# A fused transformer block with routed experts: the end of full attention in another order, and the second experts' output scatters no longer ordered

## The reference, cut to what matters

```python
attn_out = _mha(x, in_proj_w, in_proj_b, out_proj_w, out_proj_b)
x = _layernorm(x + attn_out, ln1_g, ln1_b)
# _hier_moe: one expert of eight for each of the 4096 rows
gp = jax.nn.softmax(xt @ w_group + b_group, axis=-1)
ep = jax.nn.softmax(elog, axis=-1)            # 2 experts in each of 4 groups
flat_e = g_idx * EXPERTS_PER_GROUP + e_idx_local
combine = jax.nn.one_hot(flat_e, E) * (g_prob * e_prob)[:, None]
h = jax.nn.relu(jnp.einsum('td,edf->etf', xt, w1) + b1[:, None, :])
y = jnp.einsum('etf,efd->etd', h, w2) + b2[:, None, :]
out = jnp.einsum('te,etd->td', combine, y)
x = _layernorm(x + moe_out, ln2_g, ln2_b)     # and the block's input is added once more
```

## Time and profile before

| | |
|---|---|
| median of 3 runs | 2338.34 us (2334.56 to 2341.31) |
| profiled execution | 2331.83 us, its span 2330.0 us |
| mean granted TensorE clock | 0.946 of full speed |
| PE busy over the span | 1995.3 us, 86% |
| DVE, ACT, POOL busy | 64%, 53%, 49% |

### The profile page before, as it was taken

How to read it: one execution, slowest core, us unless ns; L and a number is a source line. 1 busy time by engine, 2 the same in 40 slices (tenths; PEclk the granted TensorE clock), 3 DMA queues, 4 the chain that set the end, 5 groups by cost and what they waited for, 6 DMA issues and landing times. The chain is left out here.

```text
span 2330.0 us, 36967 instructions
## 1 busy us (share of the span) xinstructions
PE 1995.3 (86%) x12360; PEld 1189.0 (51%) x12360; DVE 1484.8 (64%) x3224; ACT 1244.2 (53%) x2953; POOL 1141.1 (49%) x949
## 2 busy tenths in 40 slices
PE   7999999989999999975677995999999999764986
PEld 3555555555555555552245783444444444333875
DVE  4348777786868687775844654666777776453555
ACT  6676666666666666742112331566666666431432
POOL 2007566584747475673663534233344432144655
PEclk9999999999999999997798996899999999985999
DMA  8214453526200000005134653123233211214653
GB/s 285 58 56 156 143 158 123 178 96 213 70 24 1 20 1 19 1 17 146 54 113 129 186 174 88 48 72 84 60 84 89 68 54 32 69 44 145 218 188 114
DMA packets 195685, 226.07 MB, mean 97 GB/s; under 512 B 24173, under 2 KB 167021, under 8 KB 195370
## 3 DMA queue, kind: packets, MB, share of 16 engines
q1 hardware_dynamic: 146250, 149.48, 21.3%
q0 software_dynamic: 14880, 39.35, 5.5%
q10 hardware_dynamic: 34368, 34.87, 4.4%
HBM read 97.92 MB, written 114.46 MB: 91 GB/s over the span
## 5 line engine op out<-in xcount | busy, mean ns | idle before, releaser
L2043 DVE TENSOR_REDUCE m_mx<-ps 128x2 f32<-128x1024 f32 x256 | 313.3, 1224 | 191.6 <-PE ps L1978 189.1
L734 DVE CUSTOM_DVE_ANT_0 pb<-ps,bias,snl 128x128 f32<-128x128 f32 (+3 forms) x512 | 260.2, 546 | 226.6 <-PE ps L579 225.7
L852 POOL TENSOR_TENSOR prod<-qs,kvs 128x1024 f32<-128x1024 f32 x120 | 283.9, 2393 | 163.5 <-issue 142.3
L2113 ACT ACTIVATE m_pt<-ps 128x1024 f32<-128x1024 f32 x256 | 261.4, 1023 | 171.4 <-PE ps L1986 166.6
L852 POOL TENSOR_TENSOR prod<-sc,kvs 128x1024 f32<-128x1024 f32 x120 | 280.3, 2369 | 98.5 <-ACT sc L970 85.7
L930 ACT ACTIVATE pb<-pb,mst 128x129 f32<-128x129 f32 (+3 forms) x512 | 283.4, 560 | 19.1 <-DVE mst L734 17.0
L579 PE MATMUL ps<-kz,qT 64*128 64x128 f32 (+3 forms) x1024 | 186.3, 442 | 0.0
L590 PE MATMUL ps<-ident,pb 128*128 128x128 f32 x1280 | 179.3, 279 | 0.5 <-DVE mst L734 0.4
L864 DVE TENSOR_REDUCE sc<-prod 128x64 f32<-128x1024 f32 x128 | 152.2, 1209 | 42.0 <-POOL prod L852 41.7
L945 ACT ACTIVATE ptb<-ps 128x384 f32<-128x384 f32 (+1 forms) x256 | 135.4, 544 | 67.5 <-PE ps L590 67.1
L590 PEld LDWEIGHTS ps<-ident,pb 128*128 128x128 f32 x1280 | 140.4, 142 | 55.9 <-issue 43.5
(11 more groups left out here) (337 smaller groups left out, 4273.5 us busy)
## 6 DMA issues: line engine op xcount, KB each, us to landing
xh_scratch<-zh SPq DMA_DIRECT2D x32, 1032.0 KB, 9.7
xe_scratch<-zh ACTq DMA_DIRECT2D x32, 1024.0 KB
hw_w<-in_w SPq DMA_DIRECT2D x47, 512.0 KB
...
```

Source lines behind the costliest of these rows:

```text
L734: dv.tensor_tensor_reduce(pb.ap[:, j, SEG[t]:SEG[t] + n], rS.of(("S", b, p, t, j)).ap[:, 0:n], k.bias[:, h, CAUSAL[t]:CAUSAL[t + 1]], -1.0 ...
L852: e.tensor_tensor(out, one, two, ALU.mult).then_inc(*k.c.did(*product_done(step, b, t, u)))
L2043: dv.tensor_reduce(x.ap[:, t, 64 * half:64 * half + 64].rearrange("p (i r) -> p i r", i=2)[:, :, 2], score_ring(k, b, g, t, half).of((b, g ...
L2113: ac.activation(p.ap[:, 2 * half:2 * half + 2, :], k.qE.of((b, g, kt, half)).ap, ACT.Exp).then_inc(*did("m_exp", b, g, kt, half))
```

## The change: what it does

Four edits.

1. The order of steps in `last_rows`: the four `f_out` of batch 7 stand together, then its four `f_norm`, `h_turn` and `h_score`; only then follow `h_gate` 1 and `h_count` 1 (batch 6), and `h_back` of batch 7. Before, `h_gate` 1 stood behind the second `f_out`, and `h_score` of batch 7 behind `h_count` 1.
2. The scatter of slot n to the output waits for its own rows alone.
3. `hslots` neither moves the last tile of an expert back nor repeats the last slot: tiles start at whole multiples of 128 rows of their expert's list, and what lies behind the list's end are the zero rows, whose number is out of bounds, so that gather and scatter skip them. Six DVE instructions go. The scratch has 8 tiles more, and one more `clear` of 1 MB is issued in the first part.
4. In the fourth part, `h_more` stands behind the loads of the first three slots instead of ahead of them.

```diff
@@ -305,7 +305,7 @@
 
 FOLD_AT = 4
 
-HROWS = 6
+HROWS = E8 * CAP + (NS_H - NN + 1) * P
 
 
 def order_one():
@@ -502,9 +502,10 @@
             sync_rest(k, sp)
         elif step == "clear":
             w.wait_ge(at("zero", 1))
-            i, n = key[0], E8 * CAP // CLEARS
-            sp.dma_start(k.xhd[i * n:(i + 1) * n, :].rearrange("(n p) d -> p n d", p=P),
-                         k.zh[:, :].unsqueeze(1).broadcast_to([P, n // P, ROW])).then_inc(*did("d_zh", i))
+            n = E8 * CAP // CLEARS
+            for i in range(key[0], HROWS // n, CLEARS):
+                sp.dma_start(k.xhd[i * n:(i + 1) * n, :].rearrange("(n p) d -> p n d", p=P),
+                             k.zh[:, :].unsqueeze(1).broadcast_to([P, n // P, ROW])).then_inc(*did("d_zh", i))
         elif step == "x_last":
             for t in range(NT):
                 sp.dma_start(x1_tile(k, NB - 1, t), ins["x"][NB - 1, t * P:(t + 1) * P, :]).then_inc(*did("d_xl", t))
@@ -1742,9 +1743,9 @@
     some = lambda n: [next(lots) for _ in range(n)]
     out = [("h_score", b - 1)] + [("f_turn", b, t) for t in range(NT)] + [("h_back", b - 1)]
     out += [("f_bias", b, 2)] + some(3) + [("f_bias", b, 3)] + some(6) + [("f_out", b, 0)] + some(1)
-    out += [("f_out", b, 1), ("h_gate", 1), ("f_norm", b, 0)] + some(1)
-    out += [("f_out", b, 2), ("f_norm", b, 1)] + some(1) + [("f_out", b, 3), ("f_norm", b, 2), ("f_norm", b, 3)]
-    return out + [("h_turn", b), ("h_count", 1)] + list(lots) + [("h_scatter", n) for n in range(*HLOT[1])]
+    out += [("f_out", b, t) for t in (1, 2, 3)] + [("f_norm", b, 0)] + some(1) + [("f_norm", b, 1)] + some(1)
+    out += [("f_norm", b, 2), ("f_norm", b, 3), ("h_turn", b), ("h_score", b), ("h_gate", 1), ("h_count", 1), ("h_back", b)]
+    return out + list(lots) + [("h_scatter", n) for n in range(*HLOT[1])]
 
 
 def order_three():
@@ -1754,7 +1755,7 @@
     out += [("p_v", 0, 0), ("p_v", 0, 1), ("m_banks",)] + period(-1)
     for b in range(NB + 1):
         out += period(b)
-    out += [("h_score", NB - 1), ("h_back", NB - 1), ("h_gate", HLAST), ("h_count", HLAST)]
+    out += [("h_gate", HLAST), ("h_count", HLAST)]
     return out + [("h_scatter", n) for n in range(*HLOT[HLAST])] + [("h_slots",)]
 
 
@@ -2193,7 +2194,7 @@
 
 
 def order_four():
-    return [("h_more",)] + [("h_expert", j) for j in range(NS_H + 4)] + [("h_end",)]
+    return [("h_expert", 0), ("h_more",)] + [("h_expert", j) for j in range(1, NS_H + 4)] + [("h_end",)]
 
 
 def setup_four(k, nc, ins):
@@ -2207,7 +2208,6 @@
     k.hcum = [[e["v0"](f"h_cum{g}{i}", [P, n1 - n0, E8]) for i in range(3)] for g, (n0, n1) in enumerate(HLOT)]
     k.hmore = e["v0"]("h_more", [P, E8, NN])
     k.hin = e["v0"]("h_in", [P, NS_H, E8])
-    k.hin2 = e["q"]("h_in2", [P, NS_H, E8])
     k.htot = e["v0"]("h_tot", [P, HLAST + 4, E8])
     k.hte = e["v0"]("h_te", [P, 5, NS_H])
     k.hgix = e["v0"]("h_gix", [P, NS_H], I32)
@@ -2274,7 +2274,7 @@
                 if n < NS_H:
                     x = k.hxs.of(n)
                     w.wait_ge(at("hgix", 0), at("i_hsc", NN - 1), x.room)
-                    r = sp.value_load(k.hgix[0:1, n:n + 1], min_val=0, max_val=E8 * CAP - P)
+                    r = sp.value_load(k.hgix[0:1, n:n + 1], min_val=0, max_val=HROWS - P)
                     sp.dma_start(x.ap[:, :], k.xhd[bass.ds(r, P), :]).then_inc(*did(f"d_hxs{n % HX}", n))
                     t = k.w1.take(n, at("h_h", n, 3))
                     w.wait_ge(at("h_tei", 0), t.room)
@@ -2446,7 +2446,7 @@
 def hslots(k, dv, w):
 
     did = k.c.did
-    tot, nt, first, base = [k.htot[:, i, :] for i in range(HLAST, HLAST + 4)]
+    tot, nt, first = [k.htot[:, i, :] for i in range(HLAST, HLAST + 3)]
     n = HLOT[HLAST][1] - HLOT[HLAST][0]
     w.wait_ge(at("hc_more", HLAST))
     dv.tensor_tensor(tot, k.htot[:, HLAST - 1, :], k.inch[HLAST][:, n - 1, :], ALU.add).then_inc(*did("hs_tot", 0))
@@ -2460,24 +2460,16 @@
-    te, own, at_, end, slot = [k.hte[:, i, :] for i in range(5)]
-    dv.tensor_scalar(base[:, 0:1], nt[:, E8 - 1:E8], first[:, E8 - 1:E8], 1.0, ALU.add, ALU.subtract).then_inc(*did("hs_base", 0))
-    dv.scalar_tensor_tensor(tot, tot, 1.0, k.hplace[:, 0:E8], ALU.subtract, ALU.add).then_inc(*did("hs_tot", 4))
-    w.wait_ge(at("hs_base", 0))
-    dv.tensor_scalar(slot, k.hiota[:, :], base[:, 0:1], None, ALU.min).then_inc(*did("hs_slot", 0))
-    w.wait_ge(at("hs_slot", 0))
+    te, own, at_ = [k.hte[:, i, :] for i in range(3)]
+    slot = k.hiota[:, :]
-    w.wait_ge(at("hs_in", 0), at("hs_tot", 4))
+    w.wait_ge(at("hs_in", 0))
-    dv.tensor_tensor(k.hin2[:, :, :], k.hin[:, :, :], wide8(tot, NS_H), ALU.mult).then_inc(*did("hs_in2", 0))
-    w.wait_ge(at("hs_in2", 0))
-    dv.tensor_reduce(end, k.hin2[:, :, :], AX, ALU.max).then_inc(*did("hs_end", 0))
@@ -2486,9 +2478,7 @@
-    dv.scalar_tensor_tensor(own, te, float(CAP), at_, ALU.mult, ALU.add).then_inc(*did("hs_own", 3))
-    w.wait_ge(at("hs_own", 3), at("hs_end", 0))
-    dv.tensor_tensor(k.hgix[:, :], own, end, ALU.min).then_inc(*did("hgix", 0))
+    dv.scalar_tensor_tensor(k.hgix[:, :], te, float(CAP), at_, ALU.mult, ALU.add).then_inc(*did("hgix", 0))
@@ -2598,7 +2588,7 @@
             if 0 <= j - 4 < NS_H:
                 n = j - 4
 
-                w.wait_ge(at("h_res", n), at(f"i_out{(n - 1) % HZ}", n - 1) if n else None)
+                w.wait_ge(at("h_res", n))
                 po.indirect_dma_start(k.out.rearrange("b s d -> (b s) d"), bass.IndirectOffsetOnAxis(ap=k.hxs.of(n).ap[:, D + 1:D + 2].bitcast(I32), axis=0),
                                       k.hz.of(n).ap[:, :], None, bounds_check=NN * P - 1, oob_is_err=False).then_inc(*did(f"i_out{n % HZ}", n))
             if j < NS_H:
@@ -2629,7 +2619,7 @@
-        self.xhd = nc.dram_tensor("xh_scratch", [E8 * CAP, ROW], F32).ap()
+        self.xhd = nc.dram_tensor("xh_scratch", [HROWS, ROW], F32).ap()
```

## The result

| | before | after |
|---|---|---|
| median (4 runs each, on one chip) | 2336.45 us (2321.46 to 2341.31) | 2304.59 us (2297.53 to 2306.26) |
| ratio | | 0.987, 95% interval 0.9831 to 0.9909 |
| profiled execution, and its span | 2331.83, 2330.0 us | 2306.26, 2304.4 us |
| clock | 0.946 | 0.946 |

The change makes the kernel 31.9 us faster by the medians, where 40 were forecast (2298.0, range 2289 to 2314).

A forecast was written before the change was run, and what follows sets the result against it. Output scatters, each waiting for the previous landing, were taken to hold slots at 4.525 us against PE's 3.73. Terms 4.3 + 0 + 2.3 + 33.4 = 40.0 us off the 2338.3 us median gave 2298, range 2289 to 2314.

The forecast's parts named there:

- step 1: End of attention: with batch 6's gates behind batch 7's norms, batch 7's gates start 4.3 us earlier.
- Step 2: `hslots`: six small DVE instructions go, 3 us at most, but hidden beside batch 7's scatters; gain 0.
- Step 3: Fourth part's first loads: rows asked for 1.0 us earlier and landing 1.3 us sooner without the bias ahead; 2.3 us.
- step 4: Fourth part's slots: without ordered output scatters they run at PE's 3.734 us instead of 4.525; 33.4 us gained.
- first case: Fourth part: PE paces the slots, giving the full forecast of 2298 us; chance 0.62.
- third rival: End of attention: new order gains nothing, batch 6's counting delays batch 7 or DVE stops grow; 2302 us, chance 0.08.
- The lock: Slots: DVE's port lock stretches POOL; POOL or late transfers pace at 3.85 to 4.1 us; 2303 to 2312, chance 0.25.
- Crowding out: Slots: unordered scatters and gathers crowd out the first weights, making it slower than before; about 2346 us, chance 0.02.
- the wait that comes back elsewhere: Slots: result buffers wait for the scatter six slots back, so the old pace stays; 2331.7 us, chance 0.03.

The follow-up runs named there:

- mended: Changed kernel with batch 6's exponential ahead of batch 7's turning and the bias loaded right behind slot 3's rows: 2272.50 us, ratio 0.988 to the kernel before.
- before again: The kernel before, unchanged, profiled once more on another chip, where it took 2304.24 us (median of 21 runs).
- after again: The changed kernel, unaltered, run once more on another chip: 2276.91 us, ratio 0.9901 to the kernel before.
- still ordered: Changed kernel with each output scatter again waiting for the landing of the one before: 2309.88 us, ratio 1.003 to the kernel before.
- Slots only: Kernel before with only the unordered output scatters and the shorter `hslots`, both step orders as before: 2278.06 us, ratio 0.9906.
- exponential first: Changed kernel with ACT doing the exponential of batch 6's gates ahead of batch 7's turning: 2277.18 us, ratio 0.9911 to the kernel before.
- POOL more: Changed kernel with one more one-column inverse root per slot on POOL, into a buffer nobody reads: 2279.81 us.

## Why the prediction was right, and where it was not

| | predicted | first two traces | across the other runs |
|---|---|---|---|
| step 1, order (A to X) | 4.3 | 0.8 (41.4 to 40.6) | 0.6 (36.9 to 36.3 on average); mended 1.5 |
| steps 2 and 3, `hslots` and loads (X to T) | 0 and 2.3 | -2.7 (23.1 to 25.8) | -1; mended +1 |
| step 4, slots (T to E) | 33.4 | 33.3 | 21.5 to 33.0 |
| sum (A to E) | 40.0 | 31.5 | 22.4 (before again to after again), 33.2 with still ordered in place of before |

Of the 8.5 us that are missing from the sum, 3.5 are step 1's and 5.0 lie between X and T. The time fell into the range all the same, and in part that is luck: the range stands for gains of 24 to 49 us, and on the chip of after again the same change gained 20.0; both kernels were faster there, the one before by 39.6 us, the changed one by 27.7.

- **Step 4 held** in its pace (3.734 us) and its 9.3 us behind PE's end (9.4); so did the first case, PE as the pacer. The forecast counted it from H, 156.9 us to the end with 7.84 us of filling "as before": 160.8 were measured, 29.5 us gained, because the filling took 9.4 us and the slot behind it 6.0 instead of 3.7; in after again it was 157.3. Slots only and still ordered show that no other edit gives this gain. What it did not have is that the old pace is no constant: the waits for the landing made it 4.21 to 4.53 us, and 4.525 was the slow end. By medians the unordered versions gained 20 to 33 us in the later groups, 31.9 in the first.
- **Step 1 failed in one sentence**: "The gates of batch 6 themselves (5.4 us) lie beside turning and router product ... that is their cover, with 1.9 us to spare." They lie beside them on DVE and PE, but their exponential is on ACT, behind the copy of the router product. That cost 3.8 us of N to G (15.3 against 11.5). The norms' 5.0 us (4.8 predicted; 4.0 in the later groups, 11.1 to 7.1, where DVE made no stops in the old order's gates) and the 3.7 us of turning (2099.60 to 2103.26) came as worked out. The stops of 4.3 us on DVE did not vanish: they moved from the gates of batch 7 into the counts of batch 6 and stand in both first traces; in the other twelve neither place has them.
- **Step 1 also missed a second bound.** "18 at 1.265 us ... so they cost nothing" was right about the end of POOL's list (28.5 to 29.2 us behind A with the new order; 28.9 predicted; 32.4 in the first trace, where the places of batch 6 came late), but did not have the 2.4 us and more behind it. With the exponential mended that list is what the last scatters wait for. Behind a kernel without DVE's stops the new order can give 1.2 to 1.8 us there and no more: the first scatter of batch 7 stands 33.2 us behind A in before again and 33.0 in slots only, 31.4 to 31.7 in the three with the early exponential.
- **Step 2 held**: X to R is 5.0 us in slots only and 4.9 in before again, so the shorter `hslots` gives nothing.
- **Step 3 was half as large, and had the wrong load as its risk.** X to H is 10.8 us on average with the bias behind three slots and 11.9 with it ahead: 1.1 us gained, where 2.3 were forecast. The bias took 8.2 us to land instead of 4.9. The forecast asked when DVE wants the bias (it came 0.7 us late: DVE read the first product of the second weights at 2152.0; PE had it done at 2151.3), and not which rows stand behind the bias in the queue. Those of slot 3 did, PE waited 1.96 us for them and lost 1.8 more to the clock; that is the 3.8 us of H to T in the first trace; on average over the six traces H to T is 13.6 us against 11.4.
- **The third rival**, the new order gains nothing, 2302 us, chance 0.08, is the case that step 1 came nearest to (0.6 to 0.8 us), but not for the reason that it gave: in exponential first the counting of batch 6 stands in the same place, and N to G is 11.5 us, where the forecast had 11.7.
- **The lock**, the second rival: scatter and root were stretched as it feared, the gather less (1.12 us at the median instead of 1.32), and yet it set nothing. The Trainium skill (SBUF — State Buffer, section "SBUF: two separate sides") has the port pair held for the whole instruction, by a DVE operation with two SBUF inputs too when it meets a GpSimd operation that reads SBUF, and DVE has such ones in each slot (L2380, L2388). The longer rows of POOL would fit that, but no run shows it: POOL more has the same DVE work, and its root takes 0.54 us instead of 0.73. The rival's own 3.96 us a slot did not come; 3.734 was measured. Which DVE instruction holds what was not tried.
- **Crowding out, and the wait that comes back elsewhere**, the last two rivals, are excluded: no PE row of slots 4 to 38 waits, in any unordered kernel with its full products.
